# Patch embedding of a small ViT: overlapping patches summed in pairs, three products in place of four

## The reference

```python
PH, PW = (64, 25)
SH, SW = (64, 12)
nw = (W - pw) // sw + 1
cols = jnp.arange(nw)[:, None] * sw + jnp.arange(pw)[None, :]
p = x[:, :, rows, :]
p = p[:, :, :, :, cols]
p = _unfold(x, PH, PW, SH, SW)
return jax.nn.gelu(jnp.einsum('bnk,kd->bnd', p, weight) + bias, approximate=False)
...
h = _L0_tok_ref(x, L0_tok_weight, L0_tok_bias)
h = h + _L0_attn_ref(_layernorm(h, axis=-1), L0_attn_Wq, L0_attn_Wk, L0_attn_Wv, L0_attn_Wo)
```

## Time and profile before

| | us |
|---|---|
| median of 3 runs (763.07 to 769.25) | 763.96 |
| profiled execution | 764.58 |
| its span | 762.8 |
| PE busy | 645.8 (85%) |
| DVE busy | 516.0 (68%) |
| ACT busy | 312.6 (41%) |
| POOL busy | 188.6 (25%) |

### The profile page before, as it was taken

One profiled execution on the slowest core, in us unless ns is written; L12 is line 12 of the kernel. 1 busy time (PEld: TensorE's weight loads), 2 busy tenths in 40 slices (PEclk: granted clock), 3 DMA queues, 4 the chain that ended last, 5 costly groups with the idle time before them and its releaser, 6 DMA issues. The chain is left out here.

```text
span 762.8 us, 16178 instructions
## 1 busy us (share of the span) xinstructions
PE 645.8 (85%) x6175; PEld 416.5 (55%) x6175; DVE 516.0 (68%) x1531; ACT 312.6 (41%) x707; POOL 188.6 (25%) x202
## 2 busy tenths in 40 slices
PE   2899999799966999999998898998765888888884
PEld 2875655599943445454443476887663444334432
DVE  3767797476833666566756469999754767777773
ACT  0100111155423665555563445776542353344442
POOL 1000002455441104121002075886513112121000
PEclk9999999899976999999997999999855779999998
DMA  9998950000000000000000000000000000000001
GB/s 301 410 344 307 288 211 2 1 1 2 2 1 0 1 1 2 1 1 1 1 1 0 1 1 1 1 2 1 2 1 1 6 14 19 17 17 17 18 21 27
DMA packets 28125, 38.98 MB, mean 51 GB/s; under 512 B 19344, under 2 KB 19600, under 8 KB 28048
## 3 DMA queue, kind: packets, MB, share of 16 engines
q1 hardware_dynamic: 19232, 35.46, 13.1%
q10 hardware_dynamic: 8816, 2.49, 1.8%
HBM read 35.25 MB, written 2.69 MB: 50 GB/s over the span
## 5 line engine op out<-in xcount | busy, mean ns | idle before, releaser
L419 POOL TENSOR_TENSOR centred<-h,mean 82x512 f32<-82x512 f32 x64 | 66.7, 1042 | 427.5 <-DVE rstd L408 256.1
L1549 DVE TENSOR_TENSOR m_hm<-bank,m_h 128x656 f32<-128x656 f32 x112 | 93.6, 836 | 81.4 <-PE bank L1339 65.8
L1221 ACT ACTIVATE m_h<-bank,m_b 128x656 f32<-128x656 f32 x112 | 90.3, 806 | 109.1 <-PE bank L1323 73.9
L280 PE MATMUL bank<-cols,tok_weight 64*64 64x328 f32 (+1 forms) x1800 | 114.0, 409 | 17.7 <-DVE cols L318 15.8
L280 PEld LDWEIGHTS bank<-cols,tok_weight 64*64 64x64 f32 x1800 | 75.7, 135 | 52.9 <-issue 18.0
L317 DVE COPY cols<-image 128x1992 f32<-128x1992 f32 x32 | 62.1, 1949 | 17.5 <-DMA image<-in_x_dram 15.8
L421 POOL TENSOR_TENSOR xn<-centred,rstd 82x512 f32<-82x512 f32 x64 | 66.7, 1043 | 5.0
L1347 PE MATMUL bank<-m_h,m_w 128*128 128x328 f32 x192 | 66.7, 471 | 0.0
L1323 PE MATMUL bank<-m_xt,m_w 64*64 64x328 f32 x512 | 55.2, 504 | 6.4 <-ACT m_h L1221 5.0
L1359 PE MATMUL bank<-m_hm,m_wo 64*64 64x328 f32 x512 | 51.4, 470 | 6.4 <-DVE m_osb L1556 6.0
L1227 ACT ACTIVATE m_h<-bank,m_b 128x656 f32<-128x656 f32 x48 | 38.7, 807 | 37.1 <-PE bank L1347 36.9
(11 more groups left out here) (177 smaller groups left out, 1183.7 us busy)
## 6 DMA issues: line engine op xcount, KB each, us to landing
image<-in_x_dram SPq DMA_DIRECT2D x32, 1000.0 KB, 11.2
out_dram<-m_fin SPq DMA_DIRECT2D x16, 164.0 KB
tok_weight<-in_L_tok_weight_dram ACTq DMA_DIRECT2D x2, 400.0 KB, 8.5
m_w<-in_L_ffn_w_dram ACTq DMA_DIRECT2D x2, 128.0 KB
m_sel_raw<-c_sel_dram ACTq DMA_DIRECT2D x1, 256.0 KB
m_w<-in_L_ffn_expert_w_dram ACTq DMA_DIRECT2D x2, 96.0 KB
m_sel_raw<-c_sel_dram ACTq DMA_DIRECT2D x1, 192.0 KB
m_bo_raw<-in_L_ffn_expert_b_dram ACTq DMA_DIRECT2D x9, 1.5 KB
```

What stands on the lines that cost most here:

```text
L280: return pe.matmul(sum_bank[u % 2][s][t * D:(t + 1) * D, L * j0:L * j1], weight[s * R:(s + 1) * R, c, :], cols[u % 2][s * R:(s + 1) * R, c ...
L419: pool.tensor_tensor(self.centred[:], slots(self.h, g), mean.broadcast_to([L, G, D]), ALU.subtract).then_inc(self.shifted, 1)
L1221: act.activation(h1[n % RING][:], h1_bank, ACT.Gelu if last else ACT.Relu, bias=W.b1[:, k:k + 1]).then_inc(h1_ready, 1)
L1549: dve.tensor_tensor(hm[k][:], cb_bank, src[n % RING][:], ALU.mult).then_inc(hm_ready, 1)
```

## The change

Take patches in pairs: patch 2m reads blocks X0 and X1, patch 2m + 1 reads X1 and X2, with W0 and W1 the weights of a patch's first and second block. Then patch 2m is W0 (X0 - X1) + (W0 + W1) X1, and patch 2m + 1 is W1 (X2 - X1) + (W0 + W1) X1. The last term is shared, so three products of 164 columns stand for four. The 25th column is added to the first and the third. DVE makes X0 - X1 (`fore`) and X1 - X2 (`aft`, W1 with its sign turned), and once the sum of the weights; ACT copies X1 (`mid`) and the last columns (`ends`). PE multiplies `mid`, then `fore`, then `aft`. ACT copies the shared sum out of PSUM (`both`), DVE adds it to the two others (`add`), and ACT applies Gelu. ACT also stores the turned result in `h`, which DVE did. `aft` has one buffer, `fore` and `mid` two. A load still brings four images; there are five buffers for them, each free when ACT (`copied`) and DVE (`behind`) have taken it.

```diff
 UNIT = 16
 NU = B // UNIT
-NBLOCK = L + (PW - 1) // SW
+HP = L // 2
+SLOTS = 5
...
+        image = [sb(f"image{p}", [128, 2, T]) for p in range(SLOTS)]
...
+        fore = [sb(f"fore{p}", [128, SW, UNIT // 2, HP]) for p in (0, 1)]
+        mid = [sb(f"mid{p}", [128, SW, UNIT // 2, HP]) for p in (0, 1)]
+        aft = sb("aft", [128, SW, UNIT // 2, HP])
+        ends = [sb(f"ends{p}", [128, 2, UNIT // 2, HP]) for p in (0, 1)]
         weight = sb("tok_weight", [128, PW, D])
+        w_sum = sb("tok_weight_sum", [128, SW, D])
         bias = sb("tok_bias", [128, 1])
+        both = sb("tok_both", [128, 2, NPAIR * HP])
...
-        sum_bank = [banks[0:2], banks[2:4]]
         turn_bank = banks[4:6]
         w = A["L0_tok_weight"].rearrange("(r c) d -> r c d", c=PW)
         b1 = A["L0_tok_bias"].rearrange("(d a) -> d a", a=1)
+        def blocks(pairs, n):
+            first = (0, 0, SW, 2 * SW - 8)[n]
+            at = n * SW - first
+            return pairs[:, :, first:first + 2 * SW * HP].rearrange("p k (m c) -> p c k m", c=2 * SW)[:, at:at + (SW if n < 3 else 1)]
+        def sums(u):
+            return psum[:, 2 * (u % 2):2 * (u % 2) + 2, 0:3 * HALF // 2]
+        def parts(u, s):
+            return sums(u)[:, s, :].rearrange("p (a m) -> p a m", a=3)[:, 0:3:2, :]
...
+                for i in range(4 * NU):
+                    if i >= SLOTS:
+                        sp.wait_ge(behind, i - SLOTS + 1)
+                        sp.wait_ge(copied, i - SLOTS + 1)
+                    sp.dma_start(image[i % SLOTS][:], x[:, 2 * i:2 * i + 2, :]).then_inc(loaded[i % SLOTS], 16)
...
+                def copy(u, q):
+                    i, k = 4 * u + q, 2 * q
+                    act.wait_ge(loaded[i % SLOTS], i // SLOTS * 16 + 16)
+                    if u >= 2:
+                        act.wait_ge(summed, u - 1)
+                    src = image[i % SLOTS][:]
+                    act.activation(mid[u % 2][:, :, k:k + 2, :], blocks(src, 1), ACT.Copy)
+                    for a in (0, 1):
+                        ins = act.activation(ends[u % 2][:, a, k:k + 2, :], blocks(src, 2 + a)[:, 0], ACT.Copy)
+                    ins.then_inc(copied, 1)
+                for q in range(4):
+                    copy(0, q)
                 for u in range(NU):
+                    if u + 1 < NU:
+                        for q in range(4):
+                            copy(u + 1, q)
                     act.wait_ge(summed, u + 1)
-                    if u >= 2:
-                        act.wait_ge(turned, u - 1)
+                    if u >= 1:
+                        act.wait_ge(added, 2 * u)
+                    act.activation(both[:], sums(u)[:, :, HALF // 2:HALF], ACT.Copy).then_inc(shared, 1)
+                    if u >= 1:
+                        store(u - 1)
                     for s in (0, 1):
-                        act.activation(fm[u % 2][s][:], sum_bank[u % 2][s][:, 0:HALF], ACT.Gelu, bias=bias[:]).then_inc(activated, 1)
+                        act.wait_ge(added, 2 * u + 1 + s)
+                        act.activation(fm[u % 2][s][:], fm[u % 2][s][:], ACT.Gelu, bias=bias[:]).then_inc(activated, 1)
                     for W in LOAD_IN.get(u, ()):
                         (*attn, *moe)[W].load(act)
                     for g in (2 * u, 2 * u + 1):
                         LayerNorm.after_act(act, g, None, following)
+                store(NU - 1)
...
+                def products(u, at, weights, tile, n, more):
+                    for c in range(n):
+                        for s in (0, 1):
+                            for t in (0, 1):
+                                pe.matmul(sums(u)[t * D:(t + 1) * D, s, HALF // 2 * at:HALF // 2 * (at + 1)], weights[s * R:(s + 1) * R, c, :],
+                                          tile[s * R:(s + 1) * R, c, t:UNIT // 2:2, :], start=(c == 0), stop=(c == n - 1 and not more))
+                def last_column(u, at, a):
+                    for s in (0, 1):
+                        for t in (0, 1):
+                            mm = pe.matmul(sums(u)[t * D:(t + 1) * D, s, HALF // 2 * at:HALF // 2 * (at + 1)], weight[s * R:(s + 1) * R, PW - 1, :],
+                                           ends[u % 2][s * R:(s + 1) * R, a, t:UNIT // 2:2, :], start=False, stop=True)
+                    return mm
...
                 for u in range(NU):
+                    if u >= 2:
+                        pe.wait_ge(added, 2 * u - 2)
                     if u == 0:
-                        for j in (0, 2):
-                            pe.wait_ge(parted, j + 2)
-                            for c in range(PW):
-                                for s in (0, 1):
-                                    for t in (0, 1):
-                                        mm = window(u, c, s, t, j, j + 2)
-                    else:
-                        pe.wait_ge(parted, 4 * u + 4)
-                        if u >= 2:
-                            pe.wait_ge(activated, 2 * u - 2)
-                        for c in range(PW):
-                            for s in (0, 1):
-                                for t in (0, 1):
-                                    mm = window(u, c, s, t, 0, NPAIR)
+                        pe.wait_ge(weighted, 2)
+                    pe.wait_ge(copied, 4 * u + 4)
+                    products(u, 1, w_sum, mid[u % 2], SW, False)
+                    pe.wait_ge(parted, 4 * u + 4)
+                    products(u, 0, weight[:, 0:SW, :], fore[u % 2], SW, True)
+                    last_column(u, 0, 0)
+                    pe.wait_ge(behind, 4 * u + 4)
+                    products(u, 2, weight[:, SW:2 * SW, :], aft, SW, True)
+                    mm = last_column(u, 2, 1)
                     mm.then_inc(summed, 1)
...
+                def part(u, q):
+                    i, k = 4 * u + q, 2 * q
...
-                def store(u):
-                    dve.wait_ge(turned, u + 1)
+                    src = image[i % SLOTS][:]
+                    dve.tensor_tensor(fore[u % 2][:, :, k:k + 2, :], blocks(src, 0), blocks(src, 1), ALU.subtract).then_inc(parted, 1)
+                def part_behind(u, q):
+                    i, k = 4 * u + q, 2 * q
+                    if u >= 1:
+                        dve.wait_ge(summed, u)
+                    src = image[i % SLOTS][:]
+                    dve.tensor_tensor(aft[:, :, k:k + 2, :], blocks(src, 1), blocks(src, 2), ALU.subtract).then_inc(behind, 1)
...
+                def add(u):
+                    dve.wait_ge(shared, u + 1)
+                    if u >= 2:
+                        dve.wait_ge(turned, u - 1)
                     for s in (0, 1):
-                        ins = dve.tensor_copy(h[:, UNIT * u + s:UNIT * u + UNIT:2, :], turn_bank[s][0:L, :].rearrange("p (b d) -> p b d", d=D))
-                    ins.then_inc(stored, 1)
+                        dve.tensor_tensor(fm[u % 2][s][:].rearrange("p (m a) -> p a m", a=2), parts(u, s),
+                                          both[:, s, :].unsqueeze(1).broadcast_to([128, 2, NPAIR * HP]), ALU.add).then_inc(added, 1)
...
+                for q in range(4):
+                    part(0, q)
+                    part_behind(0, q)
+                    if q == 0:
+                        dve.wait_ge(weights, 2 * 16)
+                        dve.tensor_tensor(w_sum[:], weight[:, 0:SW, :], weight[:, SW:2 * SW, :], ALU.add).then_inc(weighted, 1)
+                        dve.wait_ge(weighted, 1)
+                        dve.tensor_scalar(weight[:, SW:2 * SW, :], weight[:, SW:2 * SW, :], -1.0, None, ALU.mult).then_inc(weighted, 1)
...
                 for u in range(NU):
                     if u + 1 < NU:
-                        for i in range(4):
-                            part(2 * u + 2 + i // 2, i % 2)
+                        for q in range(4):
+                            part(u + 1, q)
+                    if u + 1 < NU:
+                        for q in range(4):
+                            part_behind(u + 1, q)
+                    add(u)
                     if u >= 1:
-                        store(u - 1)
                         statistics(2 * u - 2)
                         statistics(2 * u - 1)
...
-                store(NU - 1)
```

More of the change, by code:

```diff
@@ L163, in build, with layer_norm, normalised @@
         shared = (h, stats, mean, rstd, tmp, centred)
-        xn = [[sb(f"xn{i}{p}", [L, G * D]) for p in range(3)] for i in (0, 1)]
-        norm = [LayerNorm(sem, f"ln{i}", shared, xn[i % 2], i == 1) for i in range(4)]
-        stage_patches(nc, A, banks, h, stats, ident, ident16, attn, moe, norm[0])
+        def layer_norm(i, xn):
+            return LayerNorm(sem, f"ln{i}", shared, xn, i == 1)
+        def normalised(i):
+            return [sb(f"xn{i}{p}", [L, G * D]) for p in range(3)]
+        xn = [normalised(0)]
+        norm = [layer_norm(0, xn[0])]
+        stage_patches(nc, A, psum, banks, h, stats, ident, ident16, attn, moe, norm[0])
+        xn.append(normalised(1))
```

(16 more changed lines are left out.)

18 lines of the change are left out of this document (6 added, 12 removed).

## The result

| | before | changed |
|---|---|---|
| median of the runs, us | 763.83 (763.07 to 769.25) | 836.78 (834.86 to 844.28) |
| ratio, 95% interval | | 1.0957 (1.0873 to 1.104) |
| the profiled execution, us | 764.58 | 836.57 |
| its span, us | 762.8 | 834.8 |
| next stage starts at, us | 145.44 | 219.37 |

Each column has four runs; those before are the three of the first table and one more. The change costs 73 us, three times the forecast of 24. All of it lies in the patch stage: 73.9 us between the two starts of the next stage, and the later stages take 2.0 us less than they took.

The account below looks back on a forecast made before the run. PE was taken to set the pace in seven of eight patch units. The unit-by-unit chain moved the next stage from 145.4 to 169.1 us; those 23.7 us on the profiled 764.6 gave 788, range 770 to 806 (8 in 10).

Parts of the forecast that it names:

- first product starts: Patch unit 0: constants land at 13.9 us, four ACT copies follow, so PE begins at 19.5 us.
- later waits of PE for copies and differences: Patch units 2, 3, 4 and 7: PE waits 8.7, 14.6, 8.6 and 3.5 us, 35.4 in all.
- slow products after waits: PE restarts in the patch stage: 1.3 us lost at each of four, 5.2 in all.
- short instructions ("issue"): PE's 164-column products wait for instructions: 1.9, 0.7 or 1.5 us a unit, 10.4 in all.
- products of a unit at full clock: PE in each patch unit: 304 records at 35 ns, 10.6 us, in place of 14.02.
- tail: Last patch unit's sum to the next stage: about the same as before, 7.2 us.
- the price of the re-ordering: Patch stage, 984 elements: a DVE difference takes 1.17 us, an ACT copy 0.98, small copies 0.2 each.
- the prediction's chain: Patch stage, unit by unit: Gelu, weight-load issues, copies, then PE's products; the stage ends at 169.1 us.
- The prediction's own signs of being wrong: PE waiting for DVE or DMA, differences over 1.3 us, copies over 1.2 us, or copies running while ACT's queue issues.
- The third rival: Wide steps cost double on DVE and ACT in the patch stage: some 32 us more, 820 us; chance 0.06.
- ACT's lists: Weight-load issues after the Gelus of units 0, 1 and 2 hold ACT's copies: 10, 20 and 14 us taken.
- The clock: PE after a long wait: granted clock 0.50, a restart costing between nothing and 2.7 us, 1.3 taken.

Follow-up runs that it names:

- e4: Changed kernel with every re-ordering read of the images made contiguous on both DVE and ACT, other values computed: 781.50 us, ratio 1.0251.
- e2: Changed kernel with the later stages' weight loads issued from GpSimd's queue at the start, none from ACT's: 829.69 us, ratio 1.0866.
- e5: Changed kernel with contiguous image reads on DVE and ACT and the weight loads issued from GpSimd's queue: 764.38 us, ratio 1.0004.
- e7: Changed kernel with contiguous image reads on DVE alone, ACT's copies and the lists kept: 811.97 us, ratio 1.0633.
- p1: Kernel before, with a block ahead of the patch stage timing copies and differences at various steps on DVE and ACT: 803.3 us, block included.
- v1: Version with the reference's result: DVE and ACT each copy half the columns once, differences read contiguously on GpSimd and DVE, SP issues lists: 817.63 us, ratio 1.0677.
- e1: Changed kernel reading the images 12 elements apart in place of 24, other values computed: 809.63 us, ratio 1.0608.
- e3: Changed kernel reading 12 elements apart, with the weight loads issued from GpSimd's queue: 798.23 us, ratio 1.0426.

## Why the prediction was off

The direction, the place and the order of events were right; the time was 49 us short. The stage was forecast to end at 169.1 and ended at 219.4. By the prediction's own terms:

| term | forecast | measured | difference |
|---|---|---|---|
| first product starts | 19.5 | 26.6 | +7.1 |
| later waits of PE for copies and differences | 8.7 + 14.6 + 8.6 + 3.5 = 35.4 | 64.6 (ACT) + 9.1 (DVE) = 73.7 | +38.3 |
| slow products after waits | 4 x 1.3 = 5.2 | 16.9, eight times | +11.7 |
| short instructions ("issue") | 2 x 1.9 + 3 x 0.7 + 3 x 1.5 = 10.4 | none | -10.4 |
| products of a unit at full clock | 8 x 10.6 | 8 x 10.9 | +2.4 |
| tail | 7.2 | 6.8 | -0.4 |

The differences make 48.7 of 50.3 us; the attention's products behind units 2 and 3 are most of the rest. The slow products are in part an effect of the waits: four restarts were forecast, eight came.

**The step that failed is the price of the re-ordering**: "A tensor-tensor takes ... 1.03 ns an element, so 1.17 us" and "A copy takes ... so 0.98 us for 984". Measured were 2.55 and 2.58, and of the small copies 0.3 us each with overlap in place of 0.2. These prices alone make an error of this size: the prediction's chain, worked again with 2.46 to 2.49 us between starts, small copies at 0.29 and lists at 9.6, 18.2 and 11.5, ends the stage at 221.1, an estimate to set against 219.4. That it comes so near is partly luck, for the chain keeps 10.4 us of "issue" that didn't come and has 11.7 us too little of slow products. The cleaner sign is e4: with prices as forecast the time comes out 6.5 us under 788. The prediction's own signs of being wrong, "differences over 1.3 us, copies over 1.2 us", were both there.

**Why it failed**: from "The copy of today reads 12 elements (48 bytes) apart and runs at 1949/1992 = 0.98 ns an element, no slower than a contiguous operand" I concluded that steps are free. The contiguous operands beside it belonged to other operations, with two sources or on ACT. A DVE copy of one source is faster than those to begin with (0.68 us for 984), so it could lose 0.35 us to the step and look normal; a difference goes from 1.18 (e4) to 1.85 at a step of 12 and to 2.54 at 24, ACT's copy from 1.01 to 1.89 and 2.58. The Trainium skill (VectorE: DVE Perf Modes, Mode 2×_2P) says that a one-source SBUF copy can use both read ports for one tensor and a tensor_tensor can't; the ordering of 0.68 and 1.18 us agrees. The third rival, "wide steps cost double", was the case that happened, with a chance of 0.06. Its 820 was short because it priced a difference at 2.2 us and a load's copies at 2.3 against 2.5 and 3.1, and left out the clock. For it stood the rule of the Trainium skill that I set aside, and another passage that I did not weigh: the Trainium skill (Vector Engine (DVE) Microarchitecture Reference, 5.2 Measured stream behaviour on trn2) gives 2.50 to 2.51 ns a column where both sources step by 24 words. By it 984 elements cost an estimated 2.46 us; the trace agrees, with 2546 ns.

**ACT's lists**: confirmed, as to place ("issue" 8.88, 17.28 and 10.58 us before a copy) and size (9.4, 18.1, 11.4 within 10, 18 to 24 and 10 to 17, the first a little under). Single long issues such as the 2.40, 4.80 and 2.80 of the earlier trace rows are not seen now (the longest is 1.79); that SP has fewer images under way may be why, but no run shows it. The lists' share of the loss is 7 us of the whole as things stand (e2) and 17 with cheap copies (e5 against e4), both after what the longer wait between the stages takes back.

**Short instructions on PE**: the term was 0 here; PE waited 100 us for data and never for "issue". It is real all the same: e5 has 9.8 us of it against 10.4 forecast. It grows as the larger waits go: 1.4 us in e2, 1.5 in e7, 4.6 in e4.

**The clock**: the windows of PE (stretch, length, busy, granted clock, DMA share, GB/s) answer to the last line of the earlier trace rows:

```profile
26.60:33.00 6.40, 6.39 (x102) 1.00 0.70 255
...
57.20:73.20 16.00, 0.97 (x8) 0.69 0.55 175
73.20:78.40 5.20, 5.15 (x97) 0.65 1.00 326
...
86.00:105.00 19.00, 1.49 (x15) 0.62 0.45 142
105.10:111.30 6.20, 6.20 (x96) 0.53 0.95 288
```

After 16 and 19 us in which PE was busy 0.97 and 1.49, the granted clock is 0.65 and 0.53 on average over the first 96 records, near the lower level of 1.2 GHz for much of them. A restart cost 1.4 to 2.9 us, where 1.3 was taken, and there were eight. Even a wait of 2.97 us for `aft` at 50.44 was followed by such a stretch (granted clock 0.54 from 50.4 to 56.8). At PE's first start the records are as slow (6.41 us for 96), but the profile's clock reads 1.00 there, as it does at 14.93 in the earlier trace rows, from which the forecast took its 1.3; that those products are slow by the clock isn't shown.

## What to carry to other kernels

Price a strided access by the same operation on the same engine at the same step, and compare a strided row with a contiguous one of its own kind: a rate that looks normal may be a fast operation slowed down. A product saved on the bound engine is worth only what the engines that shape its operands leave of it, and here even contiguous reads with the lists out of ACT's queue (e5) left nothing, since the start, the instructions, the last unit's wait and the slow restarts took back the 25 us. Work that the bound engine waits for shouldn't stand behind a list of loads in one queue; but moving the list paid little (7 us, e2) while that work itself cost more than the bound engine's, and more (17 us, e5) when it was cheap.

## What the runs showed of the hardware

- Reading f32 a step apart, 984 elements a partition (p1; at steps of 4 and 8 one column is read twelve times over). A DVE copy takes 0.68 us contiguous, 1.01 to 1.05 at every step from 4 to 16, then 1.09, 1.17 and 1.37 at 18, 20 and 24. An ACT copy takes 1.01, then 1.84 to 1.95, then 2.03, 2.19 and 2.58. A difference on DVE, both sources stepped, takes 1.18 contiguous (e4), 1.85 at 12 and 2.54 at 24. The price is not in proportion to the step: 4 and 16 cost the same, and 24 costs more than 16. Runs of 82 in place of 41 changed nothing (1.02 on DVE, 1.89 on ACT, at step 12).
- DVE's strided copies and GpSimd's differences hold each other up: 1.34 to 3.39 us for the one, 2.30 to 4.78 for the other (v1). So do differences on both: 8.73 us for four on DVE beside 2.28 to 3.20 for one on GpSimd, or 4.45 beside 6.67.
- With the weight loads issued from GpSimd, PE's wait at the border of the two blocks grew from 2.6 us in e1 and e4 (2.99 in the changed kernel) to 4.68 in e5, 6.3 in e3 and 8.35 in e2. Why wasn't tried; it takes part of what e2, e3 and e5 gain.
